# Cross-attention with a routed feed-forward on one core: the gate's two halves in one product, one normalisation per value group, and x plus bias added by a transfer

## The reference

```
h = layernorm(x)
x = x + softmax((h Wq + bq)(ctx Wk + bk)^T / sqrt(32)) (ctx Wv + bv) Wo + bo      # 16 heads of 32
g = layernorm(x)
e = argmax(g gate_w^T)                       # 8 experts, one for each token
x = x + g expert_w[e]^T
```

## Time and profile before

| | us |
|---|---|
| median of three runs | 1034.24 |
| lowest and highest of them | 1033.22, 1035.83 |
| the profiled execution | 1033.0 |
| its span (first to last instruction) | 1031.1 |
| PE, DVE, ACT, POOL busy | 934.9, 783.3, 555.8, 546.4 |
| granted PE clock, mean | 0.947 of full speed |

### The profile page before, as it was taken

The page is one execution under the profiler, slowest core; times in us unless marked ns, Lnnn a source line. Parts: engine busy times, 40 slices in busy tenths (PEclk is TensorE's granted clock), DMA queues, the critical chain, the costliest instruction groups (busy, mean ns, idle before and its releaser), DMA issues. The chain is left out here.

```text
span 1031.1 us, 27389 instructions
## 1 busy us (share of the span) xinstructions
PE 934.9 (91%) x8834; PEld 567.6 (55%) x8835; DVE 783.3 (76%) x1802; ACT 555.8 (54%) x907; POOL 546.4 (53%) x559
## 2 busy tenths in 40 slices
PE   7475799999989999999999999999883999999996
PEld 3332466566556665566656656656562555555553
DVE  7743578999868899896899988988876565656563
ACT  4236866866748667676686676764833121212120
POOL 2431345555644546645555555454443577777774
PEclk9786899999989999998999999999987899999998
DMA  8957536455652565653645565346725355555550
GB/s 244 257 148 199 126 89 151 111 146 125 164 148 63 146 137 133 164 111 107 153 111 146 124 159 151 87 110 139 285 83 169 100 171 166 164 168 174 170 171 31
DMA packets 85686, 149.51 MB, mean 145 GB/s; under 512 B 22849, under 2 KB 24693, under 8 KB 85567
## 3 DMA queue, kind: packets, MB, share of 16 engines
q1 hardware_dynamic: 73359, 111.89, 44.0%
q0 software_dynamic: 11664, 36.05, 9.2%
q10 hardware_dynamic: 544, 0.02, 0.1%
HBM read 58.65 MB, written 40.50 MB: 96 GB/s over the span
## 5 line engine op out<-in xcount | busy, mean ns | idle before, releaser
L824 POOL TENSOR_TENSOR p_lo<-pf,p_hi 77x512 f16<-77x512 f32 x128 | 148.6, 1166 | 239.8 <-ACT p_hi L1168 239.7
L1167 ACT ACTIVATE pf<-scoresT,exp_scale 77x512 f32<-77x512 f32 x256 | 174.2, 680 | 83.5 <-PE scoresT L1002 73.0
L1474 PE MATMUL mo<-e_w,x2T_hi 128*128 x576 | 184.3, 382 | 0.7 <-DVE x2T_lo L1511 0.7
L1168 ACT ACTIVATE p_hi<-scoresT,exp_scale 77x512 f16<-77x512 f32 x256 | 174.3, 681 | 0.0
L1494 ACT ACTIVATE x2T_hi<-mt 128x512 f16<-128x512 f32 x72 | 43.0, 597 | 183.6 <-PE mt L1463 183.6
L1521 DVE SCALAR_TENSOR_TENSOR res<-mo,inv,row 128x512 f32<-128x512 f32 x72 | 54.1, 751 | 91.3 <-PE mo L1474 91.3
L1002 PE MATMUL scoresT<-q_st,k_now 97*77 97x512 f32 x256 | 105.9, 463 | 14.4 <-ACT p_hi L1168 11.2
L824 DVE TENSOR_TENSOR p_lo<-pf,p_hi 77x512 f16<-77x512 f32 x128 | 104.8, 834 | 18.3 <-ACT p_hi L1168 16.9
L1253 DVE TENSOR_REDUCE negmax<-work 128x4 f32<-128x308 f32 x256 | 112.7, 469 | 6.5 <-PE work L1050 6.4
L1474 PE MATMUL mo<-e_w,x2T_lo 128*128 x288 | 109.9, 382 | 0.0
L979 PE MATMUL work<-xnT_hi,wq_hi 128*128 128x512 f16 x256 | 101.0, 395 | 5.5 <-DVE xnT_lo L1231 5.5
(11 more groups left out here) (228 smaller groups left out, 2242.4 us busy)
## 6 DMA issues: line engine op xcount, KB each, us to landing
q_st<-q_hi SPq DMA_DIRECT2D x256, 128.0 KB, 2.4
row<-rows_by_expert SPq DMA_DIRECT2D x72, 257.5 KB, 2.9
xt<-in_x SPq DMA_DIRECT2D x16, 1024.0 KB, 7.8
q_st<-q_lo SPq DMA_DIRECT2D x128, 128.0 KB, 2.5
pay<-in_L_ffn_expert_w SPq DMA_DIRECT2D x8, 1024.0 KB, 6.9
er<-in_L_ffn_expert_w SPq DMA_DIRECT2D x7, 1024.0 KB, 15.0
k_next<-key_stacks SPq DMA_DIRECT2D x5, 462.0 KB, 9.2
key_stacks<-k_nat_hi SPq DMA_DIRECT2D x8, 154.0 KB, 3.0
```

What stands on the lines that cost most here:

```text
L824: return tt.tensor_tensor(pp[1][0:LK, g % 2, j, :], pf[:, j, :], pp[0][0:LK, g % 2, j, :], ALU.subtract)
L1167: nc.scalar.activation(pf[:, j, :], sbank[n % SB][0:LK, :], ACT.Exp, scale=exp_scale[0:LK, :])
L1168: nc.scalar.activation(pp[0][0:LK, g % 2, j, :], sbank[n % SB][0:LK, :], ACT.Exp, scale=exp_scale[0:LK, :]).then_inc(sem("exp_done"), 1)
L1474: ins = nc.tensor.matmul(obank2[u % 2][:, :], x2T[ia][:, u % 2, k, :], w, start=k == 0 and n == 0, stop=k == KT - 1 and n == 2)
```

## The change

Three edits, with the order tables adapted to them.

1. **Gate.** The hi and lo half of each gate matrix lie beside each other, so xhi or chi is multiplied by 16 columns in one matmul, and the lo half of x or c by 8 columns: 32 matmuls for a gate in place of 48. The result has 16 columns for a tile, and DVE sums the two halves with a reduction of 64 numbers to 32 in a partition first. That is one DVE instruction more at GX and one more at GC.
2. **Normalisation.** The two `pv` banks are one tensor; PV waits and signals once for a group, and V is one reciprocal of 16 and one multiplication of 512 numbers. V3 stands where V31 stood, after M33.
3. **x plus bias.** One transfer, issued by POOL, reads `bo_rep` (for all four tiles) and accumulates into `xt`. POOL's adds and their semaphore fall away. In chunk 0 this step now waits for `xn_ready` too.

```diff
-    M12 V00 V01 O2 M13 B2 Q2 R V10 V11 M20 SL P30 Q3 V20 M21 M22 M23 V21 P31 O3 M30 B3 GX VE V30 M31 M32 M33 V31
+    M12 V0 O2 M13 B2 Q2 R V1 M20 SL P30 Q3 M21 M22 M23 V2 P31 O3 M30 B3 GX VE M31 M32 M33 V3
...
-    A0 A1 A2 P02 P03 A3 P12 P13 F P22 P23 P32 P33 G D
+    A P02 P03 P12 P13 F P22 P23 P32 P33 G D
...
-            def x_plus_bo(i, t):
-                if t == 0 and not i.is_(0):
-
-                    wait_alone(pool, "xn_ready", TPC * (i.n + 1))
-                nc.gpsimd.tensor_tensor(xt[i.slot][:, t, :], xt[i.slot][:, t, :], bo_rep[:], ALU.add)\
-                    .then_inc(sem("x_plus_bo"), 1)
+            def x_plus_bo(i):
+
+                wait_alone(pool, "xn_ready", TPC * (i.n + 1))
+                nc.gpsimd.dma_start(xt[i.slot][:], bo_rep[:].unsqueeze(1).to_broadcast([P, TPC, DM]), accum_op=ALU.add)\
+                    .then_inc(sem(f"x_plus_bo{i.slot % 2}"), 16)
...
-                for h in range(2):
-
-                    pe.wait_ge(sem("normalised"), 2 * G + h + 1)
-                    for t in (2 * h, 2 * h + 1):
...
-                    ins.then_inc(sem("values_ready"), 1)
+                pe.wait_ge(sem("normalised"), G + 1)
+                for t in range(TPC):
+                    for j in range(HG):
...
+                ins.then_inc(sem("values_ready"), 1)
...
                     for t in range(TPC):
+                        col = 2 * E * t
                         for k in range(KT):
-                            ins = product(ps[:, t * E:(t + 1) * E], [v[:, k, t * P:(t + 1) * P] for v in a],
-                                          [v[:, k, :] for v in w], k == 0, k == KT - 1)
+                            if k:
+                                nc.tensor.matmul(ps[:, col:col + E], a[1][:, k, t * P:(t + 1) * P], w[:, k, 0, :],
+                                                 start=False, stop=False)
+                            ins = nc.tensor.matmul(ps[:, col:col + 2 * E], a[0][:, k, t * P:(t + 1) * P], w[:, k, :, :],
+                                                   start=k == 0, stop=k == KT - 1)
...
-            def normalise(i, g, h):
-                dve.wait_ge(sem("values_ready"), 2 * (KT * i.n + g) + h + 1 + 4)
...
+            def normalise(i, g):
+                dve.wait_ge(sem("values_ready"), KT * i.n + g + 1 + 2)
...
+            def halves(ps):
+                return ps[:, 0:TPC * 2 * E].rearrange("p (t s e) -> p t e s", t=TPC, s=2)
...
-                    do(nc.vector.tensor_tensor(gx[:, n % 2], by_tile(ps), std[:, n % 2, :].unsqueeze(2)
+                    do(nc.vector.tensor_reduce(gx[:, n % 2], halves(ps), X, ALU.add))
+                    do(nc.vector.tensor_tensor(gx[:, n % 2], gx[:, n % 2], std[:, n % 2, :].unsqueeze(2)
                                                .to_broadcast([P, TPC, E]), ALU.mult))
...
-                    return nc.vector.scalar_tensor_tensor(out=lg[:], in0=by_tile(ps), scalar=inv_gc[:], in1=gx[:, m.slot % 2],
-                                                          op0=ALU.mult, op1=ALU.add)
+                    do(nc.vector.tensor_reduce(lg[:], halves(ps), X, ALU.add))
+                    return nc.vector.scalar_tensor_tensor(out=lg[:], in0=lg[:], scalar=inv_gc[:], in1=gx[:, m.slot % 2],
+                                                          op0=ALU.mult, op1=ALU.add)
```

More of the change, by code:

```diff
@@ L99 @@
 VECTOR_LAST = order("""
-    NM C0 C1 C2 C3 O0 B0 P00 P01 O1 B1 O2 B2 P10 GC H O3 B3 VE P11 E00 E01 P20 R SL V00 V01 E02 E03 P21 E10 E11
-    V10 V11 P30 E12 E13 P31 E20 E21 V20 V21 E22 E23 V30 V31
+    NM C0 C1 C2 C3 O0 B0 P00 P01 O1 B1 O2 B2 P10 GC H O3 B3 VE P11 E00 E01 P20 R SL V0 E02 E03 P21 E10 E11 V1 P30 E12
+    E13 P31 E20 E21 V2 E22 E23 V3
 """)
@@ L244, in build @@
     wo = [sa(f"wo_{s}", [P, KT, DM], F16) for s in ("hi", "lo")]
-    gt = [sa(f"gate_{s}", [P, KT, E], F16) for s in ("hi", "lo")]
-    wg = [sa(f"wogate_{s}", [P, KT, E], F16) for s in ("hi", "lo")]
+    gt = sa("gate_h", [P, KT, 2, E], F16)
+    wg = sa("wogate_h", [P, KT, 2, E], F16)
     k_next = sa("k_next", [P, H, LK], F32R)
@@ L708, in _ @@
                 elif kind == "wg":
-                    last = lo(wg[1][:].rearrange("p k e -> p (k e)"), ps[:, 0:KT * E], scl[:, S_WG:S_WG + 1],
-                              wg[0][:].rearrange("p k e -> p (k e)"))
+                    last = lo(wg[:, :, 1, :], ps[:, 0:KT * E].rearrange("p (k e) -> p k e", k=KT),
+                              scl[:, S_WG:S_WG + 1], wg[:, :, 0, :])
                 elif kind == "bo":
@@ L769, in build @@
         sbank = [st.enter_context(nc.psum_tensor(f"scoresT{c}", [P, 512], F32)) for c in range(SB)]
-        obank = [st.enter_context(nc.psum_tensor(f"pv{c}", [P, 512], F32)) for c in range(2)]
+        obank = st.enter_context(nc.psum_tensor("pv", [P, TPC, 256], F32))
         wbank = [st.enter_context(nc.psum_tensor(f"work{c}", [P, 512], F32)) for c in range(WB)]
@@ L1010, in values @@
                 pe.wait_ge(sem("p_lo_pool"), (HG - P_DVE) * (G + 1) + HG)
-                for h in range(2):
-                    pe.wait_ge(sem("normalised"), 2 * G + h + 1)
-                    for t in (2 * h, 2 * h + 1):
-                        for j in range(HG):
-                            col = ((t % 2) * HG + j) * VC
-                            for n, (ip, iv) in enumerate(HL):
-                                ins = nc.tensor.matmul(obank[h][:, col:col + VC],
-                                                       pp[ip][:, g % 2, j, t * P:(t + 1) * P],
-                                                       v_now[iv][:, g * HG + j, :],
-                                                       start=n == 0, stop=n == 2)
-                    ins.then_inc(sem("values_ready"), 1)
+                pe.wait_ge(sem("normalised"), G + 1)
+                for t in range(TPC):
+                    for j in range(HG):
+                        for n, (ip, iv) in enumerate(HL):
+                            ins = nc.tensor.matmul(obank[:, t, j * VC:(j + 1) * VC],
+                                                   pp[ip][:, g % 2, j, t * P:(t + 1) * P], v_now[iv][:, g * HG + j, :],
+                                                   start=n == 0, stop=n == 2)
+                ins.then_inc(sem("values_ready"), 1)
             def banked(i, kind, *at):
@@ L1067, in banked @@
                     for t in range(TPC):
+                        col = 2 * E * t
                         for k in range(KT):
-                            ins = product(ps[:, t * E:(t + 1) * E], [v[:, k, t * P:(t + 1) * P] for v in a],
-                                          [v[:, k, :] for v in w], k == 0, k == KT - 1)
+                            if k:
[3 more added lines that the diff above has]
+                                                   start=k == 0, stop=k == KT - 1)
+                            if k == 0:
+                                nc.tensor.matmul(ps[:, col:col + E], a[1][:, k, t * P:(t + 1) * P], w[:, k, 0, :],
+                                                 start=False, stop=False)
                     return ins
@@ L1174, in _ @@
         def _(dve):
-            own = OwnCount(21)
+            own = OwnCount(19)
             def mark(ins):
@@ L1396, in iteration @@
                         own_parts[kind](i, *at)
-                        if (kind, *at) == ("V", KT - 1, 1) and i.slot == CPB - 1 and not i.is_(NCHUNK - 1):
+                        if (kind, *at) == ("V", KT - 1) and i.slot == CPB - 1 and not i.is_(NCHUNK - 1):
                             copy_v(i.plus(1).batch)
```

27 lines of the change are left out of this document (13 added, 14 removed).

## The result

| | before | changed |
|---|---|---|
| median of 20 runs, us | 1034.39 | 1037.51 |
| lowest and highest | 1032.97, 1035.83 | 1032.98, 1041.36 |
| profiled execution, span | 1031.1 | 1036.1 |

The changed kernel is slower here: ratio 1.0031, 95% interval 1.0020 to 1.0042. Forecast was 1032.3 with 1027.0 to 1037.5, so the time lies 0.01 us beyond the slow end of the range, on the side that had a chance of 0.16.

What follows compares the result with a forecast made beforehand. PE is nearly full, but DVE's instruction list was taken to set the turn and nearly the middle. Gains of 0.7 + 0.3 + 0.26 + 0.67 = 1.9 us from 1034.24 gave 1032.3 us, range 1027.0 to 1037.5.

Steps and rivals of the forecast that it cites:

- the side that had a chance of 0.16: Whole kernel: a measurably slower result, beyond the border of 1037.3 us; chance 0.16.
- The transfer in the first chunk: First chunk, beside expert weight loads: 4.2 to 8.4 us more engine work, up to 4 us reaching the end; chance 0.13.
- The rival that the transfer delays xt: Load of xt: the accumulating transfer shares its engines and DVE stalls, 1039.5 or up to 1087 us; chance 0.12.
- The middle: From O1's eviction to O2: O2 moves by 0 to 0.1 us, taken as 0.05, over 14 chunks 0.7 us gained.
- one of its own signs of being wrong: Middle of a chunk: the prediction is wrong if O2 comes over 0.2 us sooner after O1.
- the signal from M03 to O2: Middle: a like signal elsewhere took 0.15 us, so O2 could have come 0.06 earlier had PE been free.
- The turn: From O3's eviction to the next O0: DVE's list sets the length; change -0.02 us, over 13 turns 0.3 us gained.
- Loop turns and the end: PV3 starts 0.13 us earlier at two loop turns, 0.26; after the last chunk gate and V save 0.67.
- PE's busy time: Whole kernel: PE busy falls by 12 to 13 us and its waits for DVE grow by about 11.
- The first rival: Both gate places: the gate's saving lands on PE's path, all 12.8 us count, 1021.4 us; chance 0.12.
- the very rule on two SBUF inputs: POOL's adds: a two-SBUF-input DVE instruction contends with POOL reading SBUF; removal gives DVE up to 1.8 us a chunk.

Runs made afterwards that it cites:

- the copy: The changed kernel with the transfer's accumulation taken away, so bo_rep is copied over xt and x is left out of the sum; 1033.93 us, ratio 0.9981.
- after_3: The changed kernel, unchanged, profiled again on a second chip beside the kernel before; single time 1033.47 us, no late stretches.
- before_3: The kernel before, unchanged, profiled again on a second chip beside the changed kernel; single time 1035.05 us, two late stretches.
- late_psum: The changed kernel with the transfer issued after POOL's first two p_lo and GC's sums kept in PSUM; 1029.45 us, ratio 0.9947 to before.
- gate_only_psum: The kernel before with the gate edit alone, GC's sums kept in PSUM; 1034.23 us, ratio 0.9993.
- after_4: The changed kernel, unchanged, profiled again on a third chip beside the kernel before; single time 1040.79 us, 22 late stretches.
- before_4: The kernel before, unchanged, profiled again on a third chip beside the changed kernel; single time 1035.40 us, 25 late stretches.

## Why the prediction was wrong, point by point

**The transfer in the first chunk** is the step that failed. The prediction named the rival, doubled the work rightly (measured 6.6 us against the copy's 3.1), put up to 4 us on it, and gave it 0.13 as something that might happen, with the forecast at zero. The row for it was there: ACT waiting 6.34 us for a transfer with the engines full. A megabyte put in front of a queue that is already waited for is the forecast, not a rival. Between the pairs of profiles it measured 2.0 to 4.5 us. The work itself was sized too high, 4.2 us for a copy and 8.4 for the accumulation: what failed is that they were taken to cost nothing at a place that was already waiting.

**The transfer in the second chunk** was not in the prediction at all. I looked at what lies around the transfer in a regular chunk, where four scatters keep it behind nmT, and not at the one chunk where they are missing. It cost 1.2 to 1.9 us in three profiles and 4.2 in the fourth, where 1.7 us of half clock came on top of a wait of 2.6.

**The rival that the transfer delays xt** did not happen: no wait of DVE for xt, although the load takes 8.1 us at the median.

**The middle** was mis-sized: 0.05 forecast, 0.21 measured, 2.9 us over 14 chunks in place of 0.7. This was one of its own signs of being wrong, O2 over 0.2 us sooner after O1. DVE's side was right within 0.1 (M03's reduction 0.04 earlier against 0.05 later). The failed term is the signal from M03 to O2, which I took as 0.15 us from another place. O2 now starts 0.53 after the reduction's start, which is 0.47 and 0.06. So DVE had some 0.15 us to spare before and not 0.06, and PE was the limit there.

**The turn**: -0.02 forecast, -0.09 to -0.10 measured. The terms were right: the reduction takes 0.24 in the queue, the last V 0.89 from its start to the next instruction, and from O3's eviction to O0 it is 7.53 us against 7.55, just the forecast. The other 0.09 lies before the eviction, where I had counted nothing, and the transfer alone brings it too.

**Loop turns and the end.** 0.26 and 0.67 us were forecast. Of the 5.9 us that after_3 gains over 13 chunks on before_3, the middle and the turn make 13 x 0.31 = 4.0; the clock around the second loop turn is 1.8 more. Whether the edits bring this is not shown: the changed kernel's first profile and late_psum have 0.86 there like the kernel before. From the last nmT to the experts the kernel before takes 86.4 to 88.3 us and the changed one 87.8 each time; 0.67 cannot be read from that.

**PE's busy time** falls by 6.1 us between the first two profiles, and by 8.8 from before_3 to after_3, not by the 12 to 13 that was to show the gate's matmuls. They did go: a gate of 48 takes 1.20 us from its first start to its last, one of 32 takes 0.79. Why the busy time shows only a part of it was not followed.

**The first rival**, that all 12.8 us of the gate land on PE's path, is refuted; gate_only_psum gains nothing that can be measured.

**A risk not seen.** The reduction puts an operand of GC's instruction into SBUF. The prediction quoted the very rule on two SBUF inputs, for POOL's adds, and did not put the new instruction to it. In the changed kernel it went well by 0.05 us, by luck of the order.

**Sum.** Without late releases (after_3 against before_3): +3.1 before the first nmT, -0.5 and +1.5 to that of chunk 2, -5.9 over 13 chunks (1.8 of them the clock), -0.5 from there to the experts, and +0.8 in the experts, which no edit touches: -1.6 us, by chance near the forecast's -1.9, since a loss that was not forecast and a gain that was not forecast cancel. With them (after_4 against before_4) +7.0 up to the nmT of chunk 2, -3.3 over 13 chunks, +1.4 to the experts and +0.3 in the rest: +5.4. The difference of the first two medians, +3.1, lies between.

## What to carry to other kernels

An accumulating transfer cost the transfer engines twice what the copy did (6.6 against 3.1 us): before one replaces arithmetic on an idle engine, look for the stretch in which a transfer is already waited for, above all at the start, where the usual neighbours on its queue are missing. When an edit changes where an operand lies, put each instruction that reads it to the question who else reads SBUF at that moment. The best kernels here keep the gate and normalisation edits with the sum left in PSUM, and either leave x plus bias to POOL (1029.56 us) or issue the transfer after the first p_lo (1029.45), both 0.53% under the kernel before. The normalisation alone, at 0.37%, has an interval that overlaps theirs.

## What the runs showed of the hardware that I had not expected

- PE's signals can arrive up to 1.5 us late and in a bunch (four within 0.13 us) while its rows show no gap, in one execution of the kernel before in 25 places, in another in one.
- PE waited 2.4 and 2.6 us for one transfer in two profiles, and from 148 to 152 us its granted clock was 0.62 and 0.57. In three others it waited 1.2 to 1.9 us, and the clock was 1.00. The first two lost 4.2 us, the others just their wait.
- A DVE instruction of 0.25 us with both inputs in SBUF that starts 0.03 us behind a p_lo of POOL ends with it, after 1.17 us; 0.05 us ahead of it, it takes 0.25.
